# Ranks collected tile by tile, a round of choosing that reads PSUM, a normalisation on VectorE, and two expert halves moved, in a layer of attention and expert-choice routing

## What is computed

```python
gate_logits = einsum('bhnd,hde->bhne', xh, gate_w)        # 8 experts
t = log(clip(gate_logits, 1e-6))
for _ in range(8):                                        # sinkhorn
    t = t - logsumexp(t, axis=-2, keepdims=True)          # over the tokens
    t = t - logsumexp(t, axis=-1, keepdims=True)          # over the experts
gates = exp(t)
gv, idx = top_k(swapaxes(gates, -1, -2), 64)              # each expert takes 64 of 512 tokens
hard_gates = gv > 0.5
out = einsum('bhmei,ehio->bhmeo', xh[idx], experts) * hard_gates
y = zeros_like(xh).at[idx].set(out)                       # a token that several experts take: the last write stands
```

## Time and profile before

| | us |
|---|---|
| median of 3 runs | 494.36 |
| lowest, highest | 493.77, 494.72 |
| the profiled execution | 494.29 |
| its span, first to last instruction | 492.6 |

### The profile page before, as it was taken

The page is one execution under the profiler, slowest core; times in us unless marked ns, Lnnn a source line. Parts: engine busy times, 40 slices in busy tenths (PEclk is TensorE's granted clock), DMA queues, the critical chain, the costliest instruction groups (busy, mean ns, idle before and its releaser), DMA issues.

```text
span 492.6 us, 9354 instructions
## 1 busy us (share of the span) xinstructions
PE 422.1 (86%) x2827; PEld 206.0 (42%) x2827; DVE 396.9 (81%) x1616; ACT 320.2 (65%) x627; POOL 207.7 (42%) x387
## 2 busy tenths in 40 slices
PE   4458996998999999899999989999998976999663
PEld 3233353463445446344544634454444432434221
DVE  6977865797798879778887977988986776896997
ACT  1004684798788779878877987887777432442971
POOL 3240641564274256427525642743432210000895
PEclk9765988999999999999999999999999998999998
DMA  8770142145027004402700440270001010100122
GB/s 268 201 177 1 65 128 67 34 127 104 17 79 178 26 32 128 101 20 69 189 25 32 130 105 16 80 176 23 3 1 65 2 43 0 43 23 21 43 65 85
DMA packets 28433, 36.84 MB, mean 75 GB/s; under 512 B 2144, under 2 KB 24224, under 8 KB 26912
## 3 DMA queue, kind: packets, MB, share of 16 engines
q1 hardware_dynamic: 27312, 34.68, 25.8%
q10 hardware_dynamic: 1072, 1.57, 1.2%
HBM read 19.41 MB, written 16.78 MB: 73 GB/s over the span
## 4 chain that ended last, share of the span: by engine, by line
PE 57%; DVE 19%; ACT 13%; issue 5%; DMA 3%; POOL 1%; DVEq 1%; POOLq 0%; ACTq 0%; SPq 0%
PE PVB L496 12%; PE ROWB L471 12%; PE CHB L484 9%; PE MB L528 6%; ACT YS L744 5%; PE MB L538 5%; PE MB L504 3%; PE ROWB L630 3%; DMA YS<-parts_scratch 2%; DVE YS L1222 2%; PE CHB L630 2%; ACT XN L715 2%; ACT XN L723 2%; DVE CHB L1222 2%; PE MB L517 2%
## 5 line engine op out<-in xcount | busy, mean ns | idle before, releaser
L931 DVE CUSTOM_DVE_ANT_0 JUNK<-ROWB,TRI 128x384 bf16<-128x384 f32 (+3 forms) x512 | 220.9, 486 | 45.2 <-PE ROWB L471 43.1
L744 ACT ACTIVATE YS<-CHB 128x512 f32<-128x512 f32 x320 | 172.7, 615 | 36.9 <-PE CHB L484 35.8
L855 POOL TENSOR_SCALAR_AFFINE_SELECT YS<-YS 128x256 f32<-128x256 f32 x256 | 102.9, 408 | 166.3 <-ACT YS L744 157.6
L471 PE MATMUL ROWB<-YS 96*128 96x384 bf16 (+3 forms) x512 | 121.7, 310 | 9.6 <-issue 3.6
L484 PE MATMUL CHB<-YS 104*128 104x384 bf16 (+3 forms) x512 | 118.1, 303 | 8.7 <-ACT YS L744 5.6
L496 PE MATMUL PVB<-YS,VP 128*32 128x512 f32 (+3 forms) x1024 | 96.0, 444 | 3.2 <-POOL YS L855 3.2
L471 PEld LDWEIGHTS ROWB<-YS 96*128 96x128 bf16 x512 | 43.7, 100 | 82.3 <-issue 37.2
L484 PEld LDWEIGHTS CHB<-YS 104*128 104x128 bf16 x512 | 45.4, 98 | 48.2 <-ACT YS L744 24.8
L698 ACT ACTIVATE YS<-MB 8x1024 bf16<-8x1024 bf16 x32 | 32.5, 1016 | 36.6 <-PE MB L517 36.6
L496 PEld LDWEIGHTS PVB<-YS,VP 128*32 128x32 f32 x1024 | 32.8, 109 | 32.8 <-POOL YS L855 17.6
L931 DVE DVE_READ_ACCUMULATOR2_ANT MX<- 128x1 f32 x512 | 42.4, 83 | 0.0
(11 more groups left out here) (131 smaller groups left out, 514.3 us busy)
## 6 DMA issues: line engine op xcount, KB each, us to landing
YS<-parts_scratch SPq DMA_DIRECT2D x28, 384.0 KB, 6.9
parts_scratch<-PARTS SPq DMA_DIRECT2D x15, 384.0 KB, 2.5
parts_scratch<-PARTS SPq DMA_DIRECT2D x15, 256.0 KB, 2.1
X<-in_x SPq DMA_DIRECT2D x8, 256.0 KB, 5.6
xn_scratch<-XN2S SPq DMA_DIRECT2D x8, 256.0 KB, 2.0
XS<-xn_scratch SPq DMA_DIRECT2D x8, 256.0 KB, 2.7
out<-X SPq DMA_DIRECT2D x8, 256.0 KB, 2.3
parts_scratch<-PARTS SPq DMA_DIRECT2D x15, 128.0 KB, 1.7
```

The source lines that it names most:

```text
L471: last = pe.matmul(ROWP[BANK[u]][:, col:col + keys], QP[par][0:ROWS_K, pair, P * qb:keys], KZ[par][i % 2][0:ROWS_K, pair, 0:keys], start=T ...
L744: act.activation(PT[s % 2][:, c, :], CH[BANK[c]], ACT.Exp).then_inc(exp_done, 1)
L855: pool.affine_select(out=v, in_=v, pattern=[[0, 2], [1, P]], compare_op=ALU.is_ge, fill=0.0, base=0, channel_multiplier=-1).then_inc(causa ...
L931: last = dve.tensor_tensor_reduce(out=JUNK[BANK[u]][:, col:col + n], in0=ROWP[BANK[u]][:, col:col + n], in1=TRI[:, T - n:T], scale=1.0, sc ...
```

## The change

Four things. (1) The ranks: in place of one accumulated product of 64 x 512 and its transposition, each one-hot is used as four weights of 128 x 128, and RANKC's two columns at MID are moved through them; each product, 128 tokens x 2, goes straight to its place in MB. RT, its copy, the four transposes and two semaphores go. The tile OPEN is made ahead of the wait. (2) Of the four expert halves among the one-hots, those after the 24th and the 32nd are now issued behind the last one-hot, with the other halves. (3) The copy of the gates to GT goes; the first round reads CH[2] in PSUM. (4) Batch 7's XN2 is made by DVE (`normalize_last`), after `statistics2` and ahead of `rescale(4, 0)`, and no longer by ACT.

```diff
@@ in the list of PE
             for j in range(B * E // 2):
                 pe.wait_ge(onehot, j + 1)
-                last = pe.matmul(ROWP[2][0:B * E, :], RANKC[:, MID - 2 * j:MID - 2 * j + B * E], OH[j % 8][:, :],
-                                 start=(j == 0), stop=(j == B * E // 2 - 1)).then_inc(onehot_used, 1)
-                if j % 8 == 7:
+                for t in range(TB):
+                    last = pe.matmul(MB[:, B * E * t + 2 * j:B * E * t + 2 * j + 2], OH[j % 8][:, P * t:P * t + P],
+                                     RANKC[:, MID:MID + 2], start=True, stop=True)
+                last.then_inc(onehot_used, 1)
+                if j in (7, 15):
                     experts_next(1)
-            pe.wait_ge(rt_ready, 1)
-            for t in range(TB):
-                last = pe.transpose(MB[:, B * E * t:B * E * t + B * E], RT[:, P * t:P * t + P], IDF[0:B * E, 0:B * E])
-            last.then_inc(ranks_turned, 1)
-            experts_next(2 * (B * TB - STORED))
+            experts_next(2 * (B * TB - STORED + DENSE_HOT - 1))
@@ in the list of ACT
             for n in range(DENSE_END - 1):
                 copy_outputs(n)
-            normalize_x2(B - 1)
             xn2_taken(B - 1)
@@ in the list of DVE
+            def normalize_last():
+
+                b = B - 1
+                dve.wait_ge(misc_full, BANK_TURN["xn2T", b - 1] + 1)
+                dve.wait_ge(ln2_rstd, b + 1)
+                for t in range(TB):
+                    last = dve.tensor_scalar(XN2[:, t, :], tile_of(b, t), MV2[:, t, 0:1], RSTD2[:, t:t + 1],
+                                             ALU.subtract, ALU.mult)
+                last.then_inc(xn2_ready, 1)
...
             statistics2(B - 1)
+            normalize_last()
             rescale(4, 0, range(6))
...
             dve.wait_ge(gt_ready, 1)
-            dve.tensor_copy(GT[0][:, :], CH[2][0:B * E, :])
-            dve.drain()
             ROUNDS = TOPK // 8
             for r in range(ROUNDS):
+                values = GT[r % 2][:, :] if r > 0 else CH[2][0:B * E, :]
...
+            dve.tensor_scalar(OPEN[:, :, :], GATES[:, :, :, :].rearrange("p t b e -> p (t b) e"), 0.5, None, ALU.is_gt)
             dve.wait_ge(onehot_used, B * E // 2)
-            dve.tensor_copy(RT[:, :], ROWP[2][0:B * E, :]).then_inc(rt_ready, 1)
-            dve.tensor_scalar(OPEN[:, :, :], GATES[:, :, :, :].rearrange("p t b e -> p (t b) e"), 0.5, None, ALU.is_gt)
-            dve.wait_ge(ranks_turned, 1)
```

More of the change, by code:

```diff
@@ L251, in build @@
         OH = [sb(f"OH{i}", [P, T], BF16) for i in range(8)]
-        RT = sb("RT", [B * E, T])
         KEY = sb("KEY", [P, TB * B, E])
@@ L335, in build @@
         y_copied = sem("expert_outputs_copied")
-        rt_ready = sem("ranks_in_sbuf")
-        ranks_turned = sem("ranks_turned")
         chain = sem("weighted_sum_step")
@@ L1148, in _ @@
             dve.wait_ge(gt_ready, 1)
-            dve.tensor_copy(GT[0][:, :], CH[2][0:B * E, :])
-            dve.drain()
             ROUNDS = TOPK // 8
             for r in range(ROUNDS):
+                values = GT[r % 2][:, :] if r > 0 else CH[2][0:B * E, :]
                 if r > 0:
                     dve.wait_ge(top_removed, r)
-                dve.max(out=TOPV[r % 2][:, :], in_=GT[r % 2][:, :]).then_inc(top_found, 1)
+                dve.max(out=TOPV[r % 2][:, :], in_=values).then_inc(top_found, 1)
                 dve.wait_ge(top_found, r + 1)
@@ L1159, in _ @@
                         dve.wait_ge(top_placed, r)
-                    dve.match_replace(out=GT[1 - r % 2][:, :], in_to_replace=TOPV[r % 2][:, :], in_values=GT[r % 2][:, :],
+                    dve.match_replace(out=GT[1 - r % 2][:, :], in_to_replace=TOPV[r % 2][:, :], in_values=values,
                                       imm_value=-1.0).then_inc(top_removed, 1)
-                dve.max_index(out=TOPI[:, 8 * r:8 * r + 8], in_max=TOPV[r % 2][:, :], in_values=GT[r % 2][:, :]
+                dve.max_index(out=TOPI[:, 8 * r:8 * r + 8], in_max=TOPV[r % 2][:, :], in_values=values
                               ).then_inc(top_placed, 1)
```

## The result

The changed kernel is slower: 500.18 us median of seven runs (498.21 to 500.39), against 494.29 us for the kernel before (seven runs, 493.73 to 497.66), a ratio of 1.0099 (95% interval 1.0082 to 1.0116). The forecast was 496.6 us, with a range from 494.0 to 499.5. The direction held, the size did not: about +6 us instead of +2.3. A run more than 1.5% above the fastest of its kernel counts as slow and is left out of the ratio, which concerns one run (497.17 us, of all four parts placed anew).

A forecast was written before the change was run, and what follows sets the result against it. From 390 us the kernel was taken as a strict relay between PE and DVE. From the profiled 494.29 us, +3.4 +1.3 -0.1 -4.0 +1.7 = +2.3 gave 496.6 us, range 494.0 to 499.5.

The forecast's parts named there:

- the clock behind that wait: Before column sum 5, PE idles 4.1 us, its clock falls and two expert halves run slow: +1.3 us, between 0 and +1.7.
- the clock in the one-hots: Among and behind the one-hots, little is streamed, PE's clock falls, two halves run slow: +1.7 us, bounds 0 and +3.4.
- The wait for POOL: Last batch's normalisation on DVE waits for POOL ahead of step 4, making column sum 5 and the balancing late: +3.4 us.
- the rival by which the sum is not late: At column sum 5, the normalisation does not delay the sum: 0 in place of 3.4 and 1.3, 491.9 us; chance 2%.
- The first round from PSUM: In the choosing, DVE finishes some 0.7 us earlier without the copy, but PE's twenty halves cover it: -0.1 us.
- Ranks tile by tile: In the one-hots, 0.17 us of PE time each at 0.043 us a pair; keys at 448.13 instead of 452.10: -4.0 us.
- The rival of slow weight loads: In the one-hots, a pair costs nearer 0.111 us and PE becomes the bound: 499.5 to 504.7 us; chance 12%.
- the cover of 0.2 us: Behind the one-hots, tile 20 is ready at 451.7, DVE wants it at 451.9; covered at full clock only.
- The rival by which the clock holds there: In the one-hots, loading weights counts as work and the clock holds: 494.9 us without the 1.7; chance 25%.
- the faster rival: PE's clock never falls, neither in the gap before column sum 5 nor in the one-hots: 493.2 us; chance 10%.
- The two big terms: Late column sum 5, +3.4 us, and ranks in the one-hots, -4.1 us at full clock, said to nearly cancel.

The follow-up runs named there:

- all four parts placed anew: Changed kernel with normalisation on DVE behind step 4, 128-column filling matmul per one-hot, nineteen expert halves beside the choosing, three among the one-hots: 491.65 us, ratio 0.9944.
- the gap filled: Kernel before with only the normalisation on DVE ahead of step 4, plus four unread f32 matmuls on PE ahead of column sum 5: 498.30 us, ratio 1.0068.
- both fillings: Changed kernel plus unread matmuls: four f32 ahead of column sum 5 and one of 256 columns for each one-hot: 495.74 us, ratio 1.0006.
- the first run: Changed kernel with the last batch's normalisation back on ACT, the other parts kept: 493.83 us, ratio 0.9982.
- the last run: Changed kernel, normalisation on DVE behind step 4, nineteen halves beside the choosing, three among the one-hots, 256-column unread matmul per one-hot: 491.02 us, ratio 0.9927.

## Why the prediction was wrong

It was wrong in size. The step that failed is the price of the fallen clock: "the clock behind that wait" was put at +1.3 and measured 2.53, beyond its own bound of 1.7, and "the clock in the one-hots" was put at +1.7 and measured 2.45. A further +1.3 us lies ahead of everything that was changed. The steps themselves are found in the trace one by one.

**The wait for POOL**, +3.4: measured 3.46 in the changed kernel, with the normalisation alone and with the gap filled, 3.47 with both fillings. DVE's wait was 2.32 us, between the two rows that bounded it. That the sum and two halves would be queued behind it was right, and the rival by which the sum is not late is out.

**The clock behind that wait**, +1.3, bound +1.7: this term failed, and its bound too. That the clock falls after such a gap was right. The term counted the two halves alone. At half clock ran also the column sum ahead of them and the four transposes behind them: from the sum to the start of the transposes 4.21 us instead of 2.14 (+2.07), from there to the clipping 2.91 instead of 2.45 (+0.46). The changed kernel lost 2.53 us there; the run with the normalisation alone lost 1.70. The bound should have been the whole chain of PE's work from 396.16 to the end of the transposes of the earlier trace rows at half speed. I had also read a slow stretch as some 3 us long, from 410 to 414 before; here it was nearly 7 us, and in the run with the normalisation alone another lasted from 407 to over 420. The rule of the Trainium skill that the prediction names here (TensorE: Matmul & The Clock Gate, section HAM oscillation) speaks of idle gaps; of the two places it was held against, only this one had such a gap, 4.12 us.

**The first round from PSUM**, -0.1: measured 0.00 in the changed kernel (17.06 us in both) and nothing in the times of the run with it alone. It was hidden by the twenty halves, as said: before, PE took the token numbers 0.09 us after its last half, and it does so now, so even the 0.1 was not there. With one half moved, 0.86 us came out of it in the trace (16.2 instead of 17.06). The sum also counted the 0.1 twice, since the keys of the next term were already reckoned from a first one-hot 0.1 us earlier; without that it gives 496.7 us.

**Ranks tile by tile**, -4.0: measured -3.63, with the clock at half for a part of it. The price of a pair was put at 0.043 us, chosen between the rows on loads; it is 0.028 where nothing holds it, nearer still to the lower bound of 0.018. The rival of slow weight loads (0.111) is out. The Trainium skill (TensorE: Matmul & The Clock Gate, section Wait — 56ns, not 53.3ns?) puts the least distance of two matmuls near 25 ns however few columns they have; 28 ns for a load and its matmul, here at half clock, agrees. DVE set the pace of the one-hots more than I had it.

**The clock in the one-hots**, +1.7, bounds 0 and 3.4: mis-sized, measured 2.45 at the first select. The mechanism was the forecast one: dense work in a fifth of the time, the clock at half from about 451 to 461 us, five of the six halves that stand there slow, at least in part. I had taken two slow halves; there were four behind the keys, where the cover of 0.2 us was gone at once. The rival by which the clock holds there because PE's queue is never empty is out: in the first run PE was busy for 3.03 of the 3.10 us from its first pair to the fall. In all five traces with the ranks tile by tile and no filling the clock fell among the one-hots and stayed at half for 10.2 us or, in one, 13.7. In four of the five filled ones it did not fall there, in the fifth (both fillings) for 3.4 us. So the 128 weight loads with their short matmuls did not keep the clock in any of these executions, and the filling kept it in most.

**What no term had**, +1.3: the end of batch 7's statistics, before which nothing was changed. It lay between 391.59 and 395.32 us in the fourteen profiled executions, whose instructions are the same up to there (393.86 before, 395.32 with the PSUM round alone, 391.59 with ACT normalising), so the changed kernel's 395.16 fits a spread of the attention, near its upper end. The granted clock was lower early on (0.71 from 40 to 60 us and 0.86 from 80 to 100, where the kernel before had 0.78 and 0.93), but that isn't the whole of it: the execution of the last run was at half for as long in the attention (41 us in sum) and ended the statistics at 393.47. What sets the spread stays open, and whether the six executions without a trace had as late an end isn't known. The sum of the edits is then +4.76 us, and a forecast with the two clock terms right (2.5 and 2.5) would have been 498.6 us, inside the range. That the time left the range is in part this spread; that the range's middle was too low is the price of the clock.

What I put down as the faster rival, the clock holding at both places, was tried by force, if not quite reached (in the traced execution the clock still fell for 3.4 us in the one-hots): with both fillings the kernel comes out even, 1.0006. The two big terms do nearly cancel; most of the difference between no change and 1% slower is the clock.

## What to carry to other kernels

Before an instruction that waits is put into an in-order list, look at what stands behind it and at who waits for that: here four instructions behind one more call cost nothing, and ahead of it 3.5 us, plus the clock of the engine that they kept waiting. When work on TensorE is replaced by a cheaper form, price the work behind it at both clocks: the cheap form took 3.6 us off its own stretch and gave 2.5 back in the next, and a matmul that nobody reads for each one-hot was worth some 2 us. A gap or a thin stretch on TensorE slows everything that runs on it until the clock is back, not only the two instructions that one has in view.

## What was not expected of the hardware

A TensorE that is busy by the trace nearly all of the time can lose its clock: 32 groups of four weight loads of 128x128 bf16, each with a matmul of two columns, and halves of 0.86 us between some of the groups, left the granted clock at 0.50 in all five traces that had them alone. With 256 columns more for each group it stayed at 1.00 in two traces and fell for 3.4 us in a third; with 128 more it stayed in both. The pairs themselves did not run slower at half clock: 0.028 us each, where an estimate for the full clock gives 0.026 (the filled groups start 0.158 us apart with 128 columns more and 0.21 with 256, so 0.105 is left for four pairs).

At half clock the kernel doesn't get out at once: slow stretches of nearly 7 us (up to 406.5 in the changed kernel, TensorE busy for 5.3 of it), 10 us (451 to 461, busy throughout) and 13.7 us (407 to 420.6 in the run with the normalisation alone, busy for 12.2 of it) were seen.

Three search instructions read a 64x512 tile in PSUM as fast as in SBUF: 0.69, 0.67 and 0.68 us.
